# A mixture-of-experts layer on one core: the block table made in two parts, and part of the weight split moved to POOL

## Time and profile before

| | us |
|---|---|
| median of 3 runs (lowest, highest) | 206.79 (206.23, 207.61) |
| the profiled execution | 207.15 |
| its span, first to last instruction | 205.3 |
| busy: PE, DVE, ACT, POOL | 153.6, 160.5, 148.2, 112.3 |

### The profile page before, as it was taken

One profiled execution on the slowest core, in us unless ns is written; L12 is line 12 of the kernel. 1 busy time (PEld: TensorE's weight loads), 2 busy tenths in 40 slices (PEclk: granted clock), 3 DMA queues, 4 the chain that ended last, 5 costly groups with the idle time before them and its releaser, 6 DMA issues.

```text
span 205.3 us, 5521 instructions
## 1 busy us (share of the span) xinstructions
PE 153.6 (75%) x1466; PEld 121.7 (59%) x1466; DVE 160.5 (78%) x803; ACT 148.2 (72%) x448; POOL 112.3 (55%) x198
## 2 busy tenths in 40 slices
PE   0068979897997778805494898998998997999400
PEld 0025846765757366704141698988988986888300
DVE  2446197999997969696896279999999999899910
ACT  2458888997795693739021789999999999798520
POOL 4315140437879575363652203777777877578660
PEclk9999999999999995755579599999999999999975
DMA  5998192000110101110152202223222223111000
GB/s 138 313 395 261 23 334 91 0 0 28 31 41 28 40 26 43 41 40 26 40 158 53 56 15 57 60 60 81 60 75 80 59 72 81 53 42 28 28 12 0
DMA packets 16416, 15.75 MB, mean 77 GB/s; under 512 B 2810, under 2 KB 13142, under 8 KB 16386
## 3 DMA queue, kind: packets, MB, share of 16 engines
q1 hardware_dynamic: 13458, 10.83, 18.0%
q0 software_dynamic: 2272, 4.27, 6.6%
q10 hardware_dynamic: 656, 0.30, 0.5%
HBM read 10.52 MB, written 5.33 MB: 77 GB/s over the span
## 4 chain that ended last, share of the span: by engine, by line
PE 32%; DVE 29%; ACT 17%; issue 7%; DMA 5%; DVEq 3%; ACTq 2%; POOLq 1%; SPq 1%; POOL 0%
PE bank L458 5%; DVE hl L1145 5%; PE bank L430 4%; ACT hh L727 3%; PE bank L570 3%; PE bank L484 3%; DMA XN<-in_attn_embeddings 3%; PE bank L415 3%; ACT OUT L736 2%; DVEq L1135 2%; PE bank L560 2%; DVE Y L820 2%; DVE z L1154 2%; ACT R L623 2%; ACT xt L718 2%
## 5 line engine op out<-in xcount | busy, mean ns | idle before, releaser
L403 POOL DMA_INDIRECT out<-OUT,tok x39 | 40.5, 1039 | 28.1 <-issue 25.7
L368 POOL DMA_INDIRECT rows<-R,place x32 | 31.3, 979 | 17.2 <-DVE place L900 8.5
L570 PE MATMUL bank<-W2hl,hh 128*128 x156 | 32.5, 273 | 4.4 <-issue 2.2
L556 PE MATMUL bank<-sel,bias 96*128 96x128 bf16 x156 | 35.1, 225 | 0.0
L558 PE MATMUL bank<-xh,W1h 128*128 128x128 f16 x156 | 34.8, 223 | 0.0
L560 PE MATMUL bank<-xh,W1l 128*128 128x128 f16 x156 | 34.7, 223 | 0.0
L559 PE MATMUL bank<-xl,W1h 128*128 128x128 f16 x156 | 34.6, 222 | 0.0
L1145 DVE SCALAR_TENSOR_TENSOR hl<-bank,hh 128x512 f16<-128x512 f32 x39 | 26.9, 690 | 4.0 <-ACT hh L727 3.4
L415 PE MATMUL bank<-ones 128*128 128x512 bf16 x72 | 24.3, 445 | 6.1 <-DVEq L1135 2.7
L573 PE MATMUL bank<-W2hl,hl 128*128 x156 | 27.9, 219 | 0.0
L727 ACT ACTIVATE hh<-bank 128x512 f16<-128x512 f32 x39 | 23.3, 597 | 4.0 <-PE bank L560 3.4
(11 more groups left out here) (177 smaller groups left out, 468.2 us busy)
## 6 DMA issues: line engine op xcount, KB each, us to landing
XR<-rows SPq DMA_DIRECT2D x39, 66.0 KB, 1.9
W<-in_ffn_W SPq DMA_DIRECT2D x1, 2048.0 KB, 11.5
X<-in_attn_embeddings SPq DMA_DIRECT2D x2, 512.0 KB, 8.8
X<-in_attn_embeddings SPq DMA_DIRECT2D x1, 768.0 KB
out<-OUT,tok POOLq DMA_INDIRECT x39
XN<-in_attn_embeddings SPq DMA_DIRECT2D x2, 256.0 KB, 8.1
rows<-R,place POOLq DMA_INDIRECT x32
C<-in_constants SPq DMA_DIRECT2D x1, 428.0 KB, 4.7
```

The source lines that it names most:

```text
L368: pool.indirect_dma_start(out=rows[:, :], out_offset=bass.IndirectOffsetOnAxis(ap=place[u][:, k:k + 1], axis=0), in_=R[u][:, k, :], in_off ...
L403: pool.indirect_dma_start(out=out[:, :], out_offset=bass.IndirectOffsetOnAxis(ap=tok[k][:, 0:1], axis=0), in_=OUT[k][:, :], in_offset=None ...
L556: pe.matmul(h, bias3[:, c * P:(c + 1) * P], sel, start=True, stop=False)
L570: pe.matmul(y[:, 0:2 * D], hh[k][:, c * P:(c + 1) * P], w, start=c == 0, stop=False)
```

## The change

- **Two tables.** `first_table` gives the first `NB1` = 16 blocks from the counts of the first `U1` = 6 units, counting full blocks only (counts shifted right by 7, without rounding up). PE sums those counts inside `logits(6)`. Steps 0 to 4 stand in window 9, 5 to 7 behind it. `second_table` gives the other 23 blocks from all counts less what the first used. Its step 0 (which also gives `pad_row`) stands behind window 11; steps 1 to 9 are run two per block behind `b_bn` in the first five block rounds (`b_table`). The steps wait on the semaphore `tabled` (8 when the first table is whole, 9 after step 0 of the second, 18 at the end) in place of drains.
- **Splits.** POOL makes the W1 low halves of q = 0 and 1 in two passes each over 128 by 1024 (a product in place, then a subtraction), ahead of the scatters of units 5 and 6. DVE makes W2 of q = 0 and W1 of q = 2 behind window 9, W1 of q = 3 behind window 10, and W2 of q = 1, 2, 3 in the first rounds of the block loop (`b_split`), between the `xl` instructions of blocks 0, 1, 2 and 3.
- **Waits.** SP starts the loads at `tabled` 8 and the scatters of units 0 to 5; it reads 16 rows' numbers first. All 8 paddings are written by SP ahead of the load of block 8; ahead of that of block 16 it waits for `tabled` 18, the padding and the last scatters. ACT writes no padding and waits for no table. PE waits for `tabled` 9, runs no spins there, and `b_h` of block 0 waits for the W1 splits, `b_y` of block 0 for `split_lo`.

```
@@ POOL
+            def split_lo(q):
+                pool.wait_ge(s["split_hi"], q + 1)
+                e2 = slice(2 * q, 2 * q + 2)
+                pool.tensor_scalar(W1[:, e2, :], W1[:, e2, :], scl[:, 1:2], None, ALU.mult).then_inc(s["pool_lo"], 1)
+                pool.wait_ge(s["pool_lo"], 2 * q + 1)
+                pool.tensor_tensor(W1l[:, e2, :], W1[:, e2, :], W1h[:, e2, :], ALU.subtract).then_inc(s["pool_lo"], 1)
             for i in range(-1, NU + 4):
+                if i in (NU + 1, NU + 2):
+                    split_lo(i - NU - 1)
@@ PE
+                if u == U1:
+                    pe.wait_ge(s["counted"], U1)
+                    pe.matmul(log_ps[:, 300:300 + E], ones16[:, :], carry16[:, :], start=True, stop=True).then_inc(s["tot_ps"], 1)
...
-            spin(nT_ps[:, :], 12)
-            pe.wait_ge(s["table"], 1)
-            spin(nT_ps[:, :], 14)
-            pe.wait_ge(s["split_lo"], 1)
-            spin(nT_ps[:, :], 6)
+            pe.wait_ge(s["tabled"], READ_2)
@@ SP
-            sp.wait_ge(s["pad_rows"], 1)
-            pads(sp, 0, E // 2)
-            sp.wait_ge(s["table"], 1)
-            sp.wait_ge(padded, 16 * (E + 1))
-            for i in range(4):
-                sp.wait_ge(scattered[i], 16 * NT * (NU // 4))
+            sp.wait_ge(s["tabled"], TABLE_1)
+            for i in range(U1 // 2):
+                sp.wait_ge(scattered[i], 16 * NT * 2)
...
             load_rows(0)
+            load_rows(UN)
             for b in range(NB):
+                if b == UN:
+                    sp.wait_ge(s["tabled"], READ_2)
+                    pads(sp, 0, E // 2)
+                    pads(sp, E // 2, E // 2)
+                if b == NB1:
+                    sp.wait_ge(s["tabled"], TABLE_2)
+                    sp.wait_ge(padded, 16 * (E + 1))
+                    sp.wait_ge(scattered[3], 16 * NT * 2)
+                    load_rows(NB1)
@@ ACT
-            act.wait_ge(s["pad_rows"], 1)
-            pads(act, E // 2, E // 2)
@@ DVE
                 if i == 9:
-                    split_lo1(0)
+                    first_table(5)
                     split_lo2(0)
+                    first_table(6)
+                    first_table(7)
+                    split_lo1(2)
                 if i == 10:
-                    split_lo1(1)
+                    split_lo1(3)
...
-            split_lo2(1)
-            for q in range(2, E // 2):
-                split_lo1(q)
-                split_lo2(q)
-            dve.drain().then_inc(s["split_lo"], 1)
+            second_table(0)
+            dve.drain().then_inc(s["split_w1"], 1)
+            def b_split(count, k):
+                n = count(0) * UN + k
+                if n < 3:
+                    split_lo2(n + 1)
+                if n == 3:
+                    dve.drain().then_inc(s["split_lo"], 1)
+            def b_table(count, k):
+                n = count(0) * UN + k
+                for step in (2 * n + 1, 2 * n + 2):
+                    if step < 10:
+                        second_table(step)
...
-            steps([(1, b_hl), (-1, b_mv), (0, b_z0), (-2, b_rec), (0, b_z), (-2, b_shift), (0, b_bn), (4, b_xl)])
+            steps([(1, b_hl), (-1, b_mv), (0, b_z0), (-2, b_rec), (0, b_z), (-2, b_shift), (0, b_bn), (0, b_table), (4, b_xl), (4, b_split)])
```

`first_table` has 12 instructions in its 8 steps (the wide ones over 16 blocks by 8 experts, 128 elements a partition), `second_table` 20 in its 10 (the wide ones over 23 by 8, 184 elements), two of them in step 0. One wide instruction of each:

```
+                    tt(past[:, 0:n, :], cend[:, :].unsqueeze(1).to_broadcast([P, n, E]),
+                       C[:, C_BLK:C_BLK + n].unsqueeze(2).to_broadcast([P, n, E]), ALU.is_le).then_inc(s["tabled"], 1)
...
+                    dve.tensor_reduce(blk[:, 1, m], past2[:, m, :], AX.X, ALU.add)
+                    ts(blk[:, 0, m], blk[:, 0, m], float(E - 1), None, ALU.min).then_inc(s["tabled"], 1)
```

More of the change, by code:

```diff
@@ L42 @@
 UN = 8
+NB1, U1 = 16, 6
+NB2 = NB - NB1
+READ_1, TABLE_1, READ_2, TABLE_2 = 1, 8, 9, 18
 LN_EPS = 1e-5
@@ L156, in build @@
         place = [sb(f"place{i}", [P, NT], I32) for i in range(NU)]
-        tot = sb("tot", [P, E])
+        full = sb("full", [P, E])
+        used_end = sb("used_end", [P, E + 1])
+        used = sb("used", [P, E])
+        first = sb("first", [P, E + 1])
+        cend2 = sb("cend2", [P, E])
         nblk = sb("nblk", [P, E])
@@ L198, in build @@
                  "counted guide_sq guide_norm guided guideT_ps guideT split_hi split_lo sums sums_ps sums_read gains roots_in roots scales_w "
-                 "bias_hi bias_rest tot_ps pad_rows table pads_ready").split()
+                 "bias_hi bias_rest tot_ps tabled split_w1 pool_lo pads_ready").split()
         s = {n: sem(n) for n in names}
@@ L249, in pads @@
         def pads(eng, first, n):
-            at = [eng.alloc_register(f"pad_row{e}") for e in range(n)]
+            at = [eng.alloc_register(f"pad_row{first + e}") for e in range(n)]
             eng.load(at, pad_row[0:1, first:first + n])
@@ L312, in _ @@
             load_rows(0)
+            load_rows(UN)
             for b in range(NB):
-                if b % UN == UN // 2 and b + UN // 2 < NB:
+                if b == UN:
[7 more added lines that the diff above has]
+                    load_rows(NB1)
+                if b > NB1 and b % UN == UN // 2 and b + UN // 2 < NB:
                     load_rows(b + UN // 2)
@@ L326, in _ @@
             pool.memset(sums[:, :], 0.0)
+            pool.memset(used_end[:, 0:1], 0.0)
+            pool.memset(first[:, E:E + 1], float(PADROW))
             pool.memset(epsc[:, :], LN_EPS)
@@ L544, in b_next @@
                 if k == UN // 2 and (count(0) + 1) * UN < NB:
+                    if (count(0) + 1) * UN == NB1:
+                        pe.wait_ge(s["tabled"], TABLE_2)
                     load_experts((count(0) + 1) * UN)
@@ L566, in b_y @@
                 pe.wait_ge(every["hl"], blocks(count(0), k))
+                if count(0) * UN + k == 0:
+                    pe.wait_ge(s["split_lo"], 1)
                 for c in range(FC):
@@ L960, in window @@
                     root(5, 6)
+                if i == NU + 1:
+                    first_table(1)
                 if do_r:
@@ L976, in window @@
                     root(6, 7)
+                if i == NU + 1:
+                    first_table(2)
                 if do_r:
@@ L1107, in _ @@
[L1107 to L1112, removed]
-            dve.tensor_tensor_scan(cend[:, :], ones[:, 0:E], nblk[:, :], 0.0, ALU.mult, ALU.add)
-            ts(jump[:, :], nblk[:, :], -float(P), float(REG), ALU.mult, ALU.add)
-            dve.drain()
@@ L1124, in _ @@
-            dve.drain()
-            stt(blk[:, 2, :], C[:, C_BLK:C_BLK + NB], float(P), blk[:, 1, :], ALU.mult, ALU.add)
-            dve.tensor_copy(blk_e[:, 0:NB], blk[:, 0, :])
-            ts(sel16[:, :], blk[0:96, 0, :], C[0:96, C_EID:C_EID + 1], None, ALU.is_equal)
-            dve.drain()
-            ts(blk_row[:, 0:NB], blk[:, 2, :], float(PADROW), None, ALU.min)
-            dve.drain().then_inc(s["table"], 1)
-            split_lo2(1)
-            for q in range(2, E // 2):
-                split_lo1(q)
-                split_lo2(q)
```

94 lines of the change are left out of this document (81 added, 13 removed).

## The result

| | us |
|---|---|
| kernel before, median of 5 | 206.79 |
| changed kernel, median of 5 (lowest, highest) | 209.2 (207.66, 209.86) |
| ratio, with its 95% interval | 1.0106 [1.0056, 1.0157] |
| the changed kernel's profiled execution, its span | 207.66, 205.9 |

The change makes the kernel about 1% slower; 202.3 was forecast, with a range up to 206.0. The profiled execution is the fastest of the five, so its 0.5 us over that of before is less than the medians' difference. Medians are of all executions of a kernel, ratios of the means of those in the chip's fast state, so the two can differ a little.

The account below looks back on a forecast made before the run. Some 14 us without block work (DVE's table and splits, PE's spins), then PE, DVE and ACT all full: 7.6 - 2.3 (second table) - 0.8 (clock) = 4.5 off 207.15, 202.65; median 0.36 lower, 202.3; range 199.9 to 206.0.

Parts of the forecast that it names:

- So POOL is covered with 0.85 to spare: Start of block 0: POOL's token lets `hl` run at 109.25, while DVE gets there only at 110.1.
- a sum for DVE's windows 9 to 11: DVE ahead of the blocks: 0.5 in window 9, window 10 2.0 late, totals read at 102.7 instead of 100.92.
- The price of a split: POOL's product and subtraction for one W1 split, ahead of the scatters of units 5 and 6: 3.5 together.
- the other estimate of 3.3: POOL split priced from the Trainium skill's two-input pass, 2.25 for the subtraction, with a one-input pass near line rate.
- 100.2 + 2L: When `hh` of block 0 comes by POOL's chain, with two splits of length L each, in the slow-POOL rival (chance 0.08).
- The rival of the ports: POOL's wide passes hold DVE up in window 9 and beside the second split: 204.3, up to 207; chance 0.22.
- The rest of the chain: Start of the blocks: first `xl` at 105.6, `hl` of block 0 at 110.1, of block 2 at 114.0, 7.6 earlier.
- the register read: PE reading eight registers after `tabled` 9, formerly under the spins: 1.3 taken, between 0 and 2.1.
- Window 10: DVE's window 10 begins at 96.3 instead of 94.33, 2.0 late, behind first-table steps 5 to 7 and a split.
- The second table: Its DVE steps among the first block rounds: 0.5 for steps 1 and 2, 2.3 for steps 3 to 9.
- Paddings and SP: SP's eight paddings ahead of the load of block 8 take 6.6, from 103 to 109.6, and cost nothing.
- The clock: PE starts cold without spins, a round at half clock up to 1.9 longer: 0.8 charged, bounds 0 and 3.8.

Follow-up runs that it names:

- e3: Changed kernel with all W1 low halves made by DVE and none by POOL, nothing left out; 202.41 us, ratio 0.9897 to the kernel before.
- e6: e3 with five unused PE products added ahead of the first `b_y`; 200.15 us, ratio 0.9744 to the kernel before.
- e12: The changed kernel run again unedited, on another chip; 206.8 us, ratio 1.0057 to the kernel before.
- e10: Changed kernel with POOL's product pass alone, subtraction left out, W1 low halves of experts 0 to 3 zeros; 202.49 us, ratio 0.9853.
- e4: Kernel before with only POOL making W1 low halves of q = 0 and 1 ahead of the scatters of units 5 and 6; 211.28 us, ratio 1.0318.
- e8: e6 with POOL's token of blocks 0 to 3 moved ahead of the scatter of unit 7; 199.98 us, ratio 0.9733.

## Why the prediction was wrong

- **The failed step is "So POOL is covered with 0.85 to spare", together with a sum for DVE's windows 9 to 11 that has no term for POOL's passes.** The step asked only whether the passes fit in POOL's holes. What they do to DVE stands in the sum at nothing. The runs showed holds in its place: the passes cost 4.8 to 5.9 us of lead (35.7 with them, 30.8 and 29.8 without), where fills as long cost only 1.9. The 0.85 failed as well. The token of POOL ended the wait of the first `hh`, and DVE idled 0.71, because the places of unit 6 came late from DVE.
- **The price of a split** was 5.07 and not 3.5: 2.86 the product and 2.12 the subtraction, both inside the bounds of 1.0 to 3.0 each (which add up to 6.0, not to the 5.0 given), and above the other estimate of 3.3, mostly by the product. By the prediction's own 100.2 + 2L that alone would have put the first `hh` at 110.3 and `hl` 0.8 behind its 110.1, a small part of the loss.
- **The rival of the ports named the mechanism and was under-priced.** It got 0.22 and "some 2 likely" out of 7. Its "up to 207" is short by its own working: 202.3 and 7 are 209.3. The argument against it was a two-input DVE instruction that ran inside a POOL pass of 1.67. That pass works on 8 elements, so it says little of one that reads 1024 a partition; the cast at 0.39 beside a scatter was the row to weigh. With 5.9 for the passes the sum is 202.3 + 5.9 = 208.2, a ratio of 1.007 to the 206.79 of before, between the two measured (1.0106 and 1.0057).
- **The rest of the chain was nearly right, the time by luck.** Without POOL's passes (e3) the first `xl` is at 104.48 (105.6 forecast) and `hl` of block 0 at 109.74 (110.1). Errors cancel in it. Up to `tabled` 9 that execution took 1.4 less than forecast, mostly because DVE didn't idle at the start of window 9 as it had before, and the register read 0.1 less; the clock cost 1.4 and not 0.8. The time of e3, 202.41, looks like the 202.3 forecast, but the kernel before was faster on that chip: its gain is 1.0% (0.4 to 1.7), where 2.2% was forecast. The spans of the two profiles differ by 5.2.
- **Window 10** was forecast at 96.3; it began at 102.31, 1.3 of that the execution's own drift. The holds of 1.5, 1.6 and 1.9 (the cast of places, the product of 128 x 128, the split, each less its length alone) make 5.0. That is more than the rest of 4.7 since the forecast was 0.6 long: without passes window 10 began at 96.06 in e6, with 0.3 of drift.
- **The second table** was priced at 2.8 in all. The loop grew by 2.0 in the first profile and by 3.1 in e12, where 1.5 of it is clock (below), and moving the table out gave 1.5 back in the rounds to block 7.
- **Paddings and SP** cost nothing on the path, as said. The eight paddings took SP 8.2 and not 6.6 (from 109.64), and the load of block 8 was issued at 119.18, right behind z0 of block 0 (118.66 to 119.01).
- **The clock**: 0.8 charged, 1.4 measured in e3. The changed kernel did both: in its first profile PE was busy without a hole from 112 to 116, the granted clock was 1.00 from 116, and from `hl` of block 0 to that of block 2 it took 3.89. In e12 PE was busy for 0.79 of 2.00 from 114 to 116, the clock stayed at 0.50 until 118, and it took 5.36.

## What to carry to other kernels

Before giving an idle POOL some elementwise work, ask not only if it fits in the holes but what DVE does beside it: here 10 us of POOL work put block 0 5.9 later, more than twice the 2.4 that they saved DVE. Work that DVE can do in its own idle stretch (the two splits ahead of the first `xl`) is free where the same on the helper is not. Ask too which engine's work the helper's later steps wait for: DVE's delay came to block 0 through POOL's scatters. And a hole of 2 us of PE at the head of the loop cost 1.4 us in granted clock, though PE was only waiting in it (e6).

## What the runs showed of the hardware that I had not expected

- A one-input product over 1024 float32 on POOL took 2.86 us, longer than the two-input subtraction with a float16 result, 2.12; in pieces of 128 they took 0.67 and 0.43 each, so cutting into eight made a pair of 5.1 into 7.9 and 9.0.
- Fills, which read nothing, held DVE's short one-input instructions up to 1.16, but not its splits (1.28). POOL's product held short instructions and one of 128 x 128, but none of the splits inside it (1.27 in the changed kernel and in e10, 1.28 in e4). Only the subtraction held a split (3.15).
- The hold works the other way as well. POOL's copy of one column took 1.19 at 114.59 beside a W2 split of DVE, 0.19 by itself. That copy lies on the chain to the first `hh`; in e8, with the tokens early, the lead is 28.9 and not 29.9. A scatter in e3 took 1.89 beside two splits:

```profile
102.10 1.89 POOL L383 DMA_INDIRECT rows<-R,place  x1 [0.70 <-DVE place L917]
104.30 0.95 POOL L383 DMA_INDIRECT rows<-R,place  x1 [0.30 <-issue]
```
